# Flamingo block on one core: stacks of keys and queries that keep each bf16 part once in DRAM

## The reference

```python
q = (query @ Wq + bq).reshape(Bq, Sq, H, DK)        # Bq 8, Sq 512, H 16, DK 16
k = (key @ Wk + bk).reshape(Bq, Sk, H, DK)          # Sk 512
v = (value @ Wv + bv).reshape(Bq, Sk, H, DK)
scores = jnp.einsum('bqhd,bkhd->hbqk', q, k) / np.sqrt(DK)
attn = jax.nn.softmax(scores.reshape(H * Bq, Sq, Sk), axis=0).reshape(H, Bq, Sq, Sk)
out = jnp.einsum('hbqk,bkhd->bqhd', attn, v).reshape(Bq, Sq, H * DK)
return out @ Wo + bo
```

## Time and profile before

| what | us |
|---|---|
| median of 3 runs (lowest, highest) | 848.94 (847.61, 850.77) |
| the profiled execution's own time | 855.71 |
| its span, first to last instruction | 853.6 |
| `prepare`, about | 0 to 130 |
| `maxima`, about | 130 to 315 |
| `attend`, the stretch in which key tiles are issued | 317 to 683 |
| the rest of `attend`, and `ffn` | 683 to 853.6 |

### The profile page before, as it was taken

How to read it: one execution, slowest core, us unless ns; L and a number is a source line. 1 busy time by engine, 2 the same in 40 slices (tenths; PEclk the granted TensorE clock), 3 DMA queues, 4 the chain that set the end, 5 groups by cost and what they waited for, 6 DMA issues and landing times. The chain is left out here.

```text
span 853.6 us, 20038 instructions
## 1 busy us (share of the span) xinstructions
PE 740.9 (87%) x8129; PEld 447.5 (52%) x8151; DVE 757.1 (89%) x825; ACT 680.9 (80%) x1094; POOL 474.8 (56%) x225
## 2 busy tenths in 40 slices
PE   8897897777777769999999999999999999559977
PEld 6564372111212225677666777677777677424334
DVE  4799646999999978999999999999999995758957
ACT  3444448999999979899998999999999834759873
POOL 1233454000000000999999999999999997415500
PEclk9999998999999989999999999999999999879989
DMA  9897798766766627668867787868867794000014
GB/s 294 276 305 225 218 276 208 197 174 172 194 175 174 239 91 235 186 185 281 264 190 206 236 291 212 225 197 288 260 194 213 242 312 138 0 1 1 1 50 147
DMA packets 98442, 165.87 MB, mean 194 GB/s; under 512 B 9712, under 2 KB 37104, under 8 KB 98032
## 3 DMA queue, kind: packets, MB, share of 16 engines
q1 hardware_dynamic: 98352, 164.60, 64.3%
HBM read 134.42 MB, written 42.73 MB: 208 GB/s over the span
## 5 line engine op out<-in xcount | busy, mean ns | idle before, releaser
L1011 POOL TENSOR_TENSOR e<-e,recip 128x1792 f32<-128x1792 f32 (+3 forms) x128 | 367.9, 2919 | 19.3 <-DVE recip L1042 19.2
L963 ACT ACTIVATE e<-psY 128x512 f32<-128x512 f32 x512 | 296.3, 646 | 33.7 <-PE psY L896 28.2
L1029 DVE TENSOR_REDUCE partial<-e 128x128 f32<-128x4096 f32 (+1 forms) x80 | 283.3, 3559 | 7.2 <-ACT e L963 7.2
L896 PE MATMUL psY<-arena 128*128 128x128 bf16 x2048 | 200.6, 221 | 1.8 <-DMA arena<-k_stack 1.7
L896 PEld LDWEIGHTS psY<-arena 128*128 128x128 bf16 x2048 | 149.3, 98 | 75.8 <-issue 26.1
L699 ACT ACTIVATE copies<-ps_max 128x1024 bf16<-128x1024 f32 x189 | 175.9, 1045 | 0.6 <-PE ps_max L678 0.6
L892 PE MATMUL psY<-shift,minus 128*128 128x512 bf16 x396 | 153.1, 387 | 10.9 <-PEq L633 5.5
L715 DVE TENSOR_TENSOR high<-copies,high 128x3072 bf16<-128x3072 bf16 x63 | 109.8, 1744 | 0.0
L1002 POOL MEMSET ones_w<- 96x128 bf16 x1 | 0.2, 206 | 174.0 <-POOLq L633 174.0
L912 PE MATMUL psX<-e,arena 128*32 128x128 f32 x2048 | 76.2, 288 | 3.0 <-issue 1.3
L296 POOL TENSOR_TENSOR parts<-rest,parts 128x512 bf16<-128x512 f32 x32 | 37.5, 1177 | 73.7 <-ACT parts L440 73.6
(11 more groups left out here) (170 smaller groups left out, 1005.8 us busy)
## 6 DMA issues: line engine op xcount, KB each, us to landing
arena<-k_stack SPq DMA_DIRECT2D x256, 256.0 KB, 3.3
arena<-q_stack SPq DMA_DIRECT2D x64, 256.0 KB, 4.4
k_stack<-parts SPq DMA_DIRECT2D x40, 256.0 KB, 3.6
q_stack<-parts SPq DMA_DIRECT2D x40, 256.0 KB, 3.5
arena<-in_x_dram SPq DMA_DIRECT2D x8, 1024.0 KB, 10.8
k_stack<-k_stack SPq DMA_DIRECT2D x12, 512.0 KB, 11.4
arena<-in_ctx_dram SPq DMA_DIRECT2D x4, 1024.0 KB, 6.7
arena<-q_stack SPq DMA_DIRECT2D x8, 512.0 KB, 8.2
```

The lines of the kernel that those rows point to most:

```text
L896: last = nc.tensor.matmul(bank[:, j * P:(j + 1) * P], ks[:, i % KRING, b * P:(b + 1) * P], qs[:, h, b * P:(b + 1) * P], start=False, stop= ...
L963: nc.scalar.activation(e_at(p, half * HB, (half + 1) * HB).rearrange("p q z i -> p z q i"), ps[n % SCORES][:].rearrange("p (z q i) -> p z ...
L1011: nc.gpsimd.tensor_tensor(part, part, by_pairs(recip[:, r % 2, :], share), ALU.mult).then_inc(pool_scaled, 1)
L1029: nc.vector.tensor_reduce(partial[:, :, k, :], e[:, t:t + n].rearrange("p t q z i -> p q i t z"), AX.XY, ALU.add).then_inc(sum_done, 1)
```

## The change

In DRAM a stack now has 48 rows for a head, each part once (`WRITES = 3` transfers a unit), and the copies from DRAM to DRAM are gone. A reader that needs eight blocks reads some parts several times: a key tile in two transfers, a query tile in three, and `load_pair` takes a 64-row piece in two transfers for keys (32 rows each) and four for queries (16 rows each). The order of the blocks in a tile changes, the pairs of parts that meet are the same. The waits are for as many times 16 as there are transfers.

```diff
-K_PARTS = (0, 0, 1, 1, 2, 2, 0, 1)
-Q_PARTS = (0, 1, 0, 1, 0, 1, 2, 2)
-K_WRITTEN = (0, 1, 2, 3, 4)
-Q_WRITTEN = (0, 1, 2, 3, 6)
-WRITES = len(K_WRITTEN)
...
+K_PLAN = ((0, 2, 3), (0, 1, 2))
+Q_PLAN = ((0, 3, 1), (1, 3, 1), (2, 2, 1))
+K_MAX_PLAN = ((0, 2), (0, 2))
+Q_MAX_PLAN = ((0, 1), (0, 1), (1, 1), (1, 1))
+WRITES = 3
+
+def repeated(sp, tile, rows, plan, loaded):
+    at = 0
+    for first, times, parts in plan:
+        n = parts * DK
+        one = rows[first * DK:first * DK + n].rearrange("(a p) x -> a p x", a=1)
+        sp.dma_start(tile[at:at + times * n], one.to_broadcast([times, n, CT])).then_inc(loaded, 16)
+        at += times * n
...
-                    if p:
-                        for what in STACK_COPIES[COPIES_A_COUPLE * (p - 1):COPIES_A_COUPLE * p]:
-                            copy_rows(sp, k_stack, q_stack, what, keep["k_copied"], keep["q_copied"])
...
-                        sp.dma_start(keep["ks"][:, h, :], k_stack[0, h]).then_inc(keep["k_loaded"][h], 16)
-                    sp.dma_start(keep["qs"][:, h, :], q_stack[0, h]).then_inc(keep["q_loaded"][h], 16)
+                        load_keys(sp, k_stack, 0, h, keep["ks"][:, h, :], keep["k_loaded"][h])
+                    load_queries(sp, q_stack, 0, h, keep["qs"][:, h, :], keep["q_loaded"][h])
...
-                        sp.dma_start(ks[:, nxt % KRING, :], k_stack[nxt // H, nxt % H]
-                                     ).then_inc(k_loaded[nxt % KRING], 16)
+                        load_keys(sp, k_stack, nxt // H, nxt % H, ks[:, nxt % KRING, :], k_loaded[nxt % KRING])
```

More of the change, by code:

```diff
@@ L36, with load_keys, load_queries @@
 LOWEST = -3.0e38
-K_PARTS = (0, 0, 1, 1, 2, 2, 0, 1)
-Q_PARTS = (0, 1, 0, 1, 0, 1, 2, 2)
-K_WRITTEN = (0, 1, 2, 3, 4)
-Q_WRITTEN = (0, 1, 2, 3, 6)
-WRITES = len(K_WRITTEN)
[L45 to L65, removed]
+K_PLAN = ((0, 2, 3), (0, 1, 2))
[10 more added lines that the diff above has]
+        at += times * n
+def load_keys(sp, k_stack, kc, h, tile, loaded):
+    repeated(sp, tile, k_stack[kc, h], K_PLAN, loaded)
+def load_queries(sp, q_stack, qc, h, tile, loaded):
+    repeated(sp, tile, q_stack[qc, h], Q_PLAN, loaded)
 def bcast_rows(vec, n):
@@ L106, with rows @@
 EARLY_ITEMS = SCORES + 1
+EVEN_PIECES = len(K_MAX_PLAN) + 2 * len(Q_MAX_PLAN)
+ODD_PIECES = len(K_MAX_PLAN)
 def load_pair(sp, p, k_stack, q_stack, even, odd, both, loaded):
-    def rows(stack, h):
-        return stack[:, h, 0:HALF, :].rearrange("c p x -> p c x")
+    def rows(stack, h, plan, tile):
+        at = 0
+        for first, parts in plan:
+            sp.dma_start(tile[at:at + parts * DK], stack[:, h, first * DK:(first + parts) * DK, :].rearrange("c p x -> p c x")
+                         ).then_inc(loaded, 16)
+            at += parts * DK
     if even is not None:
-        sp.dma_start(even[0:HALF], rows(k_stack, 2 * p)).then_inc(loaded, 16)
+        rows(k_stack, 2 * p, K_MAX_PLAN, even[0:HALF])
     if both is not None:
         for j in range(2):
-            sp.dma_start(both[j * HALF:(j + 1) * HALF], rows(q_stack, 2 * p + j)).then_inc(loaded, 16)
+            rows(q_stack, 2 * p + j, Q_MAX_PLAN, both[j * HALF:(j + 1) * HALF])
     if odd is not None:
-        sp.dma_start(odd[HALF:P], rows(k_stack, 2 * p + 1)).then_inc(loaded, 16)
+        rows(k_stack, 2 * p + 1, K_MAX_PLAN, odd[HALF:P])
 def prepare(nc, sem, x, ctx_in, wq, bq, wk, bk, wv, bv, wg, wu, wd, k_stack, q_stack, keep):
@@ L275, in _ @@
                         sp.wait_ge(s["part3_ready"], 2 * (u + 1))
-                        stack, plan, written = ((k_stack, K_PARTS, K_WRITTEN), (q_stack, Q_PARTS, Q_WRITTEN))[m]
+                        stack = (k_stack, q_stack)[m]
                         h0 = dc * (H // DC)
-                        for r in written:
+                        for r in range(WRITES):
                             sp.dma_start(stack[c, h0:h0 + H // DC, r * DK:(r + 1) * DK, :].rearrange("h d x -> d h x"),
-                                         parts[:, u % GB, plan[r], :]).then_inc(stacked[u % GB], 16)
+                                         parts[:, u % GB, r, :]).then_inc(stacked[u % GB], 16)
                 for i in range(GB):
@@ L839, in load_q @@
                 def load_q(qc, h):
-                    sp.dma_start(qs[:, h, :], q_stack[bass.ds(qc, 1), h].rearrange("a p x -> (a p) x")
-                                 ).then_inc(q_loaded[h], 16)
+                    load_queries(sp, q_stack, qc, h, qs[:, h, :], q_loaded[h])
                 def store(qc, b):
@@ L1582, in flamingo_block @@
 def flamingo_block(nc, x, ctx_in, g_x, g_f, wq, bq, wk, bk, wv, bv, wo, bo, clip_x, clip_d, wg, wu, wd, out):
-    k_stack = nc.dram_tensor("k_stack", [NC, H, P, CT], BF16, kind="Internal").ap()
-    q_stack = nc.dram_tensor("q_stack", [NC, H, P, CT], BF16, kind="Internal").ap()
+    k_stack = nc.dram_tensor("k_stack", [NC, H, WRITES * DK, CT], BF16, kind="Internal").ap()
+    q_stack = nc.dram_tensor("q_stack", [NC, H, WRITES * DK, CT], BF16, kind="Internal").ap()
     keep_wT = nc.dram_tensor("keep_wT", [P, 2, DC, IC * P], BF16, kind="Internal").ap()
```

16 lines of the change are left out of this document (6 added, 10 removed).

## The result

The changed kernel takes 1753.15 us (median of 4 runs, 1751.95 to 1755.89), the kernel before 849.71. The ratio is 2.0601, with a 95% interval of 2.0545 to 2.0657. The profiled execution took 1753.33 us, its span is 1751.3.

A forecast was written before the change was run, and what follows sets the result against it. It took the busiest DMA engine to bound the changed kernel's attention: 287 us start, 1,366 for its rows, 17 for other transfers, 167 of tail and 2.1 outside the span, about 1,840 us, range 1,680 to 2,080.

The forecast's parts named there:

- How a transfer is divided: Key and query loads: transfers are cut by outermost dimension, so 2 or 3 copies use only the same lowest-numbered engines.
- Rival C: Key and query loads: two or three engines a transfer, but others each time; landing 6.7 us, total 981 us; chance 0.04.
- The work of the busiest engine: Attention loads: 50 rows a key tile and 48 a query tile, 15,872 rows of 2 KB against 2,560 before.
- The speed of one engine: Attention loads: 23.8 GB/s from a burst, 86 ns a row, so 1,366 us for the busiest engine's rows.
- The start: End of `maxima`: first key or query load issued at 287.2 us, with 0 saved in `prepare`.
- The tail: After the last key tile lands, the 167 us to the end stay as now.
- The issues at the end of `maxima`: 20 issues become 56, 27 to 29 us, done by 314 to 316; SP may be held longer by one engine's queue.
- PE's clock can't set the pace: Attention: PE's 1.4 us a step is far under the busiest engine's 5.3 us, so a lower clock couldn't bound it.
- forecast of PE's waits: Attention: PE's waits for key tiles, weight loads included, grow from 14.8 us to some 1,000.
- Share and rate: Attention: DMA share falls from 0.76 to 0.15 to 0.18, and the rate to about 60 GB/s.
- Landings: Attention: key landings go from 3.3 us to 13 us and more, each queued behind three others.
- Rival A: Attention: transfers spread over 16 engines, SP's issues cost; three stalls of some 7 us, 22 in all, total 878; chance 0.06.

The follow-up runs named there:

- 2 x 64 rows: The kernel before, with a gap in the key stacks so each key load reads 2 x 64 different rows, 2 outermost, in one transfer: 1843.71 us.
- copies inside: The changed kernel with DRAM rows reordered so repeats are an inner dimension and 48 or 16 rows are outermost: 968.78 us, ratio to before 1.1335.
- plain rows: The kernel before with every key tile in two transfers and every query tile in three, nothing repeated: 896.64 us, ratio 1.0518.
- The last version above: The kernel before with three writes a unit into full 128-row stacks, missing blocks copied inside DRAM, one transfer a tile: 848.32 us, ratio 0.9927.

## Why the prediction was right

The forecast was 1,840 us in a range of 1,680 to 2,080; 1753.15 came, in the range and 4.7% under the forecast. By its own steps:

- *How a transfer is divided.* Right, and shown: by increments (3 and 4 in place of 16), by two packets under way at once, and by the kernels with 2 x 64 rows and with copies inside, which change the outermost dimension in either direction. The range and the chances leaned on this one term, and it held. Rival C (other engines each time) fails with it: it wanted a high share and landings near 6.7 us.
- *The work of the busiest engine,* 15,872 rows. Right: changed kernel and the 2 x 64 kernel, with different row counts, give 82.3 and 82.4 ns a row, which they could not if key and query rows were on different engines.
- *The speed of one engine.* The term that was mis-sized. I took 86 ns from a burst on 16 engines of half a microsecond. With 17 us for other transfers, (1584.5 - 278.8 - 17) / 15,872 = 81.2 ns. That is 77 us less over the launch. The 17 us stay an estimate; without them it is 82.3. The packet records have a 2 KB row at 84 ns in the median both in the changed kernel and in the six microseconds of the earlier trace rows.
- *The start.* I took 0 for the saving in `prepare` and had the first load at 287.2; it was issued at 278.8, 8 us earlier. My bounds were a gain of 9 and a loss of 3. By my own sign, that `prepare` and `maxima` end within 5 us of now, this was a miss: they ended 7 and 8 us earlier.
- *The tail.* 167 us after the last landing, 166.9 measured. 278.8 + 1305.7 + 166.9 + 2 = 1753.
- *The issues at the end of `maxima`.* The barrier moved to 350.8 because SP was held by the engine's queue, as I said it might, and it needs no term of its own in the sum above.
- *PE's clock can't set the pace.* Right in that it was slower (0.62) without being the bound. My forecast of PE's waits, from 14.8 us to some 1,000, was of PE and its weight loads together, and that sum is 1,325; on PE alone it is 623. So the size was off either way, and I had not counted that part of the longer attention shows as PE's busy time (606 us and not 356).
- *Share and rate.* 0.20 and 69 GB/s, both above my 0.15 to 0.18 and 60.
- *Landings.* 12.9 us in the median from a key's first issue to its last increment, beside 3.3 before; I had said 13 and more.
- *Rival A's price,* 22 us for the issues, is the weakest number: 43 us measured with plain rows, 114 with copies inside. Its mechanism was right (SP never waits in the query parts), its 0.32 us for a key's first issue was wrong there. It changed nothing here, as SP was not the bound.

## What to carry to other kernels

Before a transfer is written with a repeat or a split, ask what its outermost dimension is. A count of 2, 3 or 4 there, even of different rows, left it that many of the 16 engines, and all such transfers were piled on the same few. Put the copies inside the rows, or cut the transfer into plain pieces, but then count SP's issues against the time of a step, stretch by stretch: a second issue a key tile cost 2.3% by itself, most of it where queries were issued too, and once SP had no time left to wait, each further issue cost some 0.5 us. A DRAM copy that was hidden cost nothing. A fall of the DMA share together with waits for transfers is the sign: here the share was 0.20 with two engines full, and 1.01 in the stretch in which memory gave 370 GB/s.

## What had not been expected

- A lone pair of engines moved a 2 KB row in 81 to 82 ns each, some 25 GB/s, beside 22.9 when all 16 were full. In the attention of before, where the prediction had 18.9, the packets of 2 KB took 109 ns in the mean, beside 88 in the six microseconds of the earlier trace rows.
- The issue of a transfer of plain rows takes SP 0.42 us (0.30 with a wait ahead). It took 0.59 to 0.60 with copies as an inner dimension, and as much for 16 x 2 different rows, so copies aren't needed for it. With 2 x 48 or 3 x 16 outermost and no full engine in its way it took 0.62 to 0.70.
- SP can run only a little ahead of a full engine: the changed kernel's first 968 rows were issued by 350, when by 81 ns a row some 880 of them had been moved, an estimate. After that the two issues of a key tile take 0.63 + 3.55 us in the median, near the 50 x 81 ns = 4.1 us that the tile takes the busiest engine.
- With three writes a unit in place of five `prepare` ended 7 us earlier (the barrier at 123 and not 130), though ACT's waits for landings had been only 7.4 us and the first pair's loads had grown to ten issues: these took 0.47 us each, not the 0.6 of the 64-row ones. The last version above, with the same three writes, ended it at 123 too.
